# A graph network on one core: chunk bases of the next stage set earlier, node groups half a turn nearer to their edges

## The reference

```python
h = jnp.maximum(_layernorm(x), 0.0); x = x + L0(h, edges, edge_attr_64)      # edge MLP, summed by node
h = jnp.maximum(_layernorm(x), 0.0); x = x + L1(h, src, dst, edge_type_8)    # typed messages, GRU per node
h = jnp.maximum(_layernorm(x), 0.0); x = x + L2(h, src, dst, edge_attr_8)    # pair interaction, summed by node
h = jnp.maximum(_layernorm(x), 0.0); x = x + L3(h, edge_index)               # two mean-aggregation layers

# L2, per edge
p1    = tanh(p @ pp_W1 + pp_b1) @ pp_W2 + pp_b2
inter = ((concat([p1[i], p1[j]]) @ pi_W1 + pi_b1) @ pi_W2 + pi_b2) @ pi_W3   # 64 x 8 values per edge
i1    = einsum('ecb,eb->ec', inter, basis)
i1    = tanh(i1 @ ii_W1 + ii_b1) @ ii_W2 + ii_b2
out   = segment_sum(i1, j)
```

## Time and profile before

| | us |
|---|---|
| median of three executions | 10330.74 |
| profiled execution | 10343.41 |
| its span | 10341.8 |
| PE busy | 5765.4 (56%) |
| DVE busy | 4372.1 (42%) |
| ACT busy | 2424.1 (23%) |
| POOL busy | 6918.9 (67%) |
| chain that ended last: POOL, PE, issue, DVE | 46%, 26%, 18%, 5% |

### The profile page before, as it was taken

One profiled execution on the slowest core, in us unless ns is written; L12 is line 12 of the kernel. 1 busy time (PEld: TensorE's weight loads), 2 busy tenths in 40 slices (PEclk: granted clock), 3 DMA queues, 4 the chain that ended last, 5 costly groups with the idle time before them and its releaser, 6 DMA issues.

```text
span 10341.8 us, 144754 instructions
## 1 busy us (share of the span) xinstructions
PE 5765.4 (56%) x32026; PEld 3576.5 (35%) x32026; DVE 4372.1 (42%) x11981; ACT 2424.1 (23%) x4618; POOL 6918.9 (67%) x7939
## 2 busy tenths in 40 slices
PE   6999996244444447999999962333333322222222
PEld 4777773222222223444444432222222211111111
DVE  6888886132323225777777751111111111111111
ACT  5999993000000002333333320000000000000000
POOL 3333331777777776777777757777777677777777
PEclk9999998555555558999999985555555555555555
DMA  3333333111111112222222211111111111111111
GB/s 104 96 97 96 97 97 118 27 29 30 29 30 29 30 29 51 61 61 61 61 61 60 60 37 27 28 28 28 28 28 28 24 27 28 28 28 28 28 28 27
DMA packets 503888, 488.54 MB, mean 47 GB/s; under 512 B 245340, under 2 KB 299425, under 8 KB 503777
## 3 DMA queue, kind: packets, MB, share of 16 engines
q0 software_dynamic: 220480, 235.58, 11.9%
q1 hardware_dynamic: 283360, 252.43, 8.4%
HBM read 427.04 MB, written 61.15 MB: 47 GB/s over the span
## 4 chain that ended last, share of the span: by engine, by line
POOL 46%; PE 26%; issue 18%; DVE 5%; ACT 1%; POOLq 1%; DVEq 1%; DMA 0%; ACTq 0%; SPq 0%
POOL mov L671 44%; PE ps L1527 5%; PE ps L1416 3%; PE ps L1390 3%; PE ps L1423 3%; PE ps L1519 3%; POOL outs L671 2%; PE ps L1546 1%; DVE scr L940 1%; PE ps L1512 1%; PE ps L1508 1%; PE ps L1537 1%; PE ps L1414 1%; PE ps L1452 1%; PE ps L1430 1%
## 5 line engine op out<-in xcount | busy, mean ns | idle before, releaser
L1390 PE MATMUL ps<-outs,mov 128*64 128x64 f32 x9984 | 1370.5, 319 | 4220.3 <-DMA mov<-tab_q,idx 1616.3
L1390 PEld LDWEIGHTS ps<-outs,mov 128*64 128x64 f32 x9984 | 1158.2, 221 | 4548.1 <-issue 4548.1
L840 DVE TENSOR_TENSOR acc<-acc,ps 64x64 f32 (+1 forms) x1664 | 354.1, 213 | 4441.8 <-PE ps L1390 4439.5
L671 POOL DMA_INDIRECT mov<-tab_msg,idx x1664 | 1578.6, 949 | 665.7 <-issue 492.3
L671 POOL DMA_INDIRECT outs<-tab_u,idx x1664 | 1590.2, 956 | 582.1 <-issue 486.4
L671 POOL DMA_INDIRECT mov<-tab_h,idx x1664 | 1573.9, 946 | 574.8 <-issue 506.6
L671 POOL DMA_INDIRECT mov<-tab_q,idx x1664 | 1573.3, 945 | 543.1 <-issue 506.6
L940 DVE TENSOR_TENSOR scr<-ps,scr 128x512 f32<-128x512 f32 x1664 | 1063.1, 685 | 368.9 <-PE ps L1519 337.3
L1527 PE MATMUL ps<-scr,w_bas 128*64 128x512 f32 x3328 | 899.9, 619 | 0.0
L634 POOL TENSOR_TENSOR scr<-outs 128x128 f32<-128x128 f32 x416 | 191.8, 461 | 816.3 <-DVE outs L850 815.5
L850 DVE TENSOR_TENSOR outs<-rel,iota_w 128x256 f32<-128x256 f32 x1664 | 705.6, 424 | 43.1 <-issue 30.1
(11 more groups left out here) (217 smaller groups left out, 8426.4 us busy)
## 6 DMA issues: line engine op xcount, KB each, us to landing
mov<-in_dst_row SPq DMA_DIRECT2D x832, 128.0 KB, 2.7
mov<-in_ea_T SPq DMA_DIRECT2D x416, 128.0 KB, 2.5
tab_msg<-outs SPq DMA_DIRECT2D x104, 256.0 KB, 2.0
mov<-tab_msg,idx POOLq DMA_INDIRECT x1664
outs<-tab_u,idx POOLq DMA_INDIRECT x1664
mov<-tab_h,idx POOLq DMA_INDIRECT x1664
mov<-tab_q,idx POOLq DMA_INDIRECT x1664
win<-tab_g SPq DMA_DIRECT2D x416, 32.0 KB, 2.4
```

The lines of the kernel that those rows point to most:

```text
L671: nc.gpsimd.indirect_dma_start(out=gat(e, u)[:, k, :], out_offset=None, in_=table, in_offset=bass.IndirectOffsetOnAxis(ap=idx[:, u, k:k + ...
L840: nc.vector.tensor_tensor(into, into, bank(banks[u % len(banks)])[0:rows, 0:W], ALU.add) \
L1390: last = mm(bank(banks[u % len(banks)])[0:width, 0:W], values(u)[:, k, :], sel(e, u)[:, k, :], start=k == 0, stop=k == TL - 1)
```

## The change

The node groups are 4.5 turns behind their edges in place of 5. Group g is taken when chunk 8g + 36 has been added. Each engine's node turns begin a turn earlier and each piece stands 4 steps later in it (2 steps in stage 2), with a third member 1 where that reaches into the next turn. The first turn with pieces is written out ahead of the loop, since late pieces have no group yet in it.

`set_windows` for the next stage now runs at the end of each stage's steps, through `drained`, before the pieces that are left over; for stage 0 it runs before the wait for the stored table. Copies of LAST and KEEP are held for those pieces. It also runs at the end of stage 4. The clearing of `win` for stage 2 stands ahead of stage 1.

```diff
-        def chunk_loop(eng, stages, kind=None, base_lag=0, per=1, nodes=None):
+        def chunk_loop(eng, stages, kind=None, base_lag=0, per=1, nodes=None, drained=None):
...
             def pieces_at(it, u):
-                for at_step, piece in pieces:
-                    if at_step == u and (not isinstance(it, int) or it - from_turn < SG):
-                        piece(it - from_turn)
+                for at_step, piece, late in pieces:
+                    if at_step == u and (not isinstance(it, int) or 0 <= it - from_turn - late < SG):
+                        piece(it - (from_turn + late))
...
             if from_turn < ITERS:
-                with eng.Fori(from_turn, ITERS) as it:
+                turn(from_turn, True)
+                with eng.Fori(from_turn + 1, ITERS) as it:
                     turn(it, True)
...
+            if drained:
+                drained()
...
-            def set_windows(e, p):
-                w0 = dve.snap((P * e + p) * 8)
-                if e > 0:
+            def set_windows(w0, first=False, pairs=False):
+                if not first:
                     dve.wait_ge(window_order, w0)
+                    nc.vector.tensor_copy(flag[:, LAST_HELD], flag[:, LAST])
+                    nc.vector.tensor_copy(flag[:, KEEP_HELD], flag[:, KEEP])
...
                 dve.wait_ge(window_order, w0 + 8)
+                nc.vector.tensor_tensor(flag[:, AT], flag[:, AT], flag[:, KEEP], ALU.mult).then_inc(window_order, 1)
+                dve.wait_ge(window_order, w0 + 9)
                 dve.sem_inc(windowed, 1)
 
+            def next_windows(e, p):
+                set_windows(dve.snap((P * e + p) * 9 + 9), pairs=e in (1, 2))
+                held[0] = True
...
-                if e == 2:
+                if e == 1:
                     for s in range(2):
                         order(nc.vector.memset(win[s * D:(s + 1) * D, :, (1 - s) * D:(2 - s) * D], 0.0))
                 with dve.Fori(0, P) as p:
-                    set_windows(e, p)
-                    turns = WAIT_TURNS + (2 if e == 2 else 1)
+                    held[0] = False
+                    turns = WAIT_TURNS + (1 if e == 2 else 0)
                     chunk_loop(dve, make(p), mybir.EngineType.DVE, ADD_LAG[e], per=2 if e == 2 else 1,
-                               nodes=(turns, pieces(p)) if pieces else None)
+                               nodes=(turns, pieces(p)) if pieces else None, drained=lambda: next_windows(e, p))
...
-                return [(2, candidate), (3, update), (7, rows_uv)]
+                return [(6, candidate), (7, update), (3, rows_uv, 1)]
...
                     wait_flow(dve, f, "ordered", t0_, g, 0)
+                    dve.sem_inc(dve_turn, 1)
...
-                return [(2, result), (3, norm3)]
+                return [(4, result), (1, norm3, 1)]
...
-                return [(2, hidden), (6, rows_q)]
+                return [(6, hidden), (2, rows_q, 1)]
...
-                return [(1, result)]
+                return [(5, result)]
...
-                chunks = g * RING + WAIT_TURNS * RING if not isinstance(g, int) or (g + WAIT_TURNS) * RING < CH else CH
+                ahead = WAIT_TURNS * RING - RING // 2
+                chunks = g * RING + ahead if not isinstance(g, int) or g * RING + ahead < CH else CH
...
-                           nodes=(WAIT_TURNS + 2, [(1, result2)]))
+                           nodes=(WAIT_TURNS + 1, [(3, result2)]))
```

More of the change, by code:

```diff
@@ L89, in build_gnn @@
         cnt = sb("cnt", [P128, NB])
-        IS_BAD, IS_FIT, STEP, AT, TMP, LAST, KEEP = (slice(n, n + 1) for n in range(7))
+        IS_BAD, IS_FIT, STEP, AT, TMP, LAST, KEEP, LAST_HELD = (slice(n, n + 1) for n in range(8))
+        KEEP_HELD = TMP
         stat = sb("stat", [P128, 4, SB])
@@ L358, in chunk_loop @@
             from_turn, pieces = nodes or (ITERS, [])
+            pieces = [piece if len(piece) == 3 else (*piece, 0) for piece in pieces]
             def step(it, u, which, base):
@@ L399, in chunk_loop @@
                     pieces_at(ITERS + n // ring, ring)
+            if drained:
+                drained()
             if pieces:
-                for it in range(ITERS + last // ring, from_turn + SG):
+                for it in range(ITERS + last // ring, from_turn + SG + 1):
                     for u in range(last % ring if it == ITERS + last // ring else 0, ring + 1):
@@ L773, in norm, with last_flag, keep_flag @@
                                                op0=ALU.max, op1=ALU.mult).then_inc(normed, 1)
-            def set_windows(e, p):
-                w0 = dve.snap((P * e + p) * 8)
-                if e > 0:
+            held = [False]
+            def last_flag():
+                return LAST_HELD if held[0] else LAST
+            def keep_flag():
+                return KEEP_HELD if held[0] else KEEP
+            def set_windows(w0, first=False, pairs=False):
+                if not first:
                     dve.wait_ge(window_order, w0)
+                    nc.vector.tensor_copy(flag[:, LAST_HELD], flag[:, LAST])
+                    nc.vector.tensor_copy(flag[:, KEEP_HELD], flag[:, KEEP])
                 nc.vector.tensor_scalar(base_n[:, :], first_f[:, :], flag[:, IS_FIT], flag[:, AT], ALU.mult, ALU.add) \
@@ L982, in _ @@
             node_loop("T0", t0)
+            order(nc.vector.memset(flag[:, AT], 0.0))
+            set_windows(0, first=True)
             edge_phase(0, edge_mlp)
@@ L1073, in update @@
                     rows = x[:, bass.ds(g * SB, SB), :]
-                    nc.vector.scalar_tensor_tensor(out=rows, in0=delta, scalar=flag[:, LAST], in1=rows,
+                    nc.vector.scalar_tensor_tensor(out=rows, in0=delta, scalar=flag[:, last_flag()], in1=rows,
                                                    op0=ALU.mult, op1=ALU.add).then_inc(f.sems["ordered"], 1)
@@ L1122, in rows_q @@
                     rows = x[:, bass.ds(g * SB, SB), :]
-                    nc.vector.scalar_tensor_tensor(out=rows, in0=q[:, :, D:2 * D], scalar=flag[:, LAST], in1=rows,
+                    nc.vector.scalar_tensor_tensor(out=rows, in0=q[:, :, D:2 * D], scalar=flag[:, last_flag()], in1=rows,
                                                    op0=ALU.mult, op1=ALU.add).then_inc(f.sems["settled"], 1)
-                return [(2, hidden), (6, rows_q)]
+                return [(6, hidden), (2, rows_q, 1)]
             def out_pieces(p):
@@ L1445, in plain @@
                     chunk_loop(pe, [(0, sum_stage(e, p, D, lambda u: gat(e, u), gathered_here(e, p), range(4, 8)))],
-                               nodes=(WAIT_TURNS, pieces(pe.snap(p * SG))))
+                               nodes=(WAIT_TURNS - 1, pieces(pe.snap(p * SG))))
             def rows_msg(j, s):
```

19 lines of the change are left out of this document (9 added, 10 removed).

## The result

| | before | after |
|---|---|---|
| median of four executions, us | 10331.08 (10329.4 to 10331.79) | 10393.95 (10392.98 to 10394.91) |
| profiled execution | 10343.41 | 10394.91 |
| PE, DVE, POOL busy | 5765.4, 4372.1, 6918.9 | 5782.8, 4374.2, 6928.9 |
| share of the last chain: POOL, PE, issue, DVE | 46, 26, 18, 5% | 46, 24, 19, 6% |

The ratio is 1.0061 (95% interval 1.0048 to 1.0074): 63 us slower. Between the two profiled executions it is 51.5 us. Busy times say nothing of it; the stages do.

The account below looks back on a forecast made before the run. POOL's gathers were taken to bound stages 1, 3 and 4, PE and DVE stage 2's turns, with stage ends exposed. Ends -24.6 and turns +74 gave +49 us: 10393 profiled, 10380 median, range 10325 to 10402.

Parts of the forecast that it names:

- ahead of stage 1's first gather: Stage 0: `set_windows` runs while DVE waits for the store, gain 3 us.
- stage 1 to 2: Group 47's update starts 2.3 us earlier and clearing and `set_windows` behind the store go; gain 9 us, bounds 7 and 15.
- stage 2: 46 turns each 1.6 us longer, +74 us, bounds 23 and 87; the stage would take about 2240 us.
- stage 2 to 3: DVE's chain after the last edge sum, with one norm moved ahead; -2 us, bounds -6 and +4.
- stage 3: Gathers were to keep 40.0 us per turn, other DVE or PE work being covered; no change.
- stage 3 to 4: Group 48 starts 7 us earlier on ACT and 4.9 us behind the store go; gain 12 us, bounds 5 and 13.
- end: End of stage 4: `set_windows` for a stage that does not exist delays group 48's result, 1.4 us later.
- The turn: Stage 2's turn end: the result delays the load of the bases, 1.6 us per turn, 46 turns, +74 us.
- z7, result, branch, load, z0: DVE's order at stage 2's turn end: z0 starts 3.6 us after z7 in place of 2.04, 1.6 us later.
- my lower bound: Stage 2's turn end: if the load could start earlier, only the result's 0.51 us shows, 23 us in all.
- The rival that the load stays covered: Stage 2's turn end costs 0 to 0.5 us, so mainly the ends count: 10306 to 10330, middle 10316; chance 0.17.
- The ends: Stage ends: -9, -12, -2, -3, 0 and +1.4 sum to -24.6 us, bounds about -37 and -8.

Follow-up runs that it names:

- before_again: The kernel before the change, with nothing changed, run and profiled again on one chip with after_again; 10331.08 us.
- after_again: The changed kernel, with nothing further changed, run again beside before on one chip; 10394.81 us, ratio 1.0061 to before.
- r_wait: The changed kernel with the wait for the result's operations moved from the turn's end to the norm, a step later; 10351.86 us, ratio 1.0005 to before.
- lag_only: The changed kernel with `set_windows` back behind the store, node groups still 4.5 turns behind; 10411.53 us, ratio 1.0064 to before.
- win_only: The changed kernel with node groups back to 5 turns behind, keeping the early `set_windows`; 10340.31 us, ratio 0.9992 to before.
- pad: The changed kernel plus one copy nobody reads in `hidden` of stage 3, to move `sel` later; 10400.73 us, ratio 1.0052 to before.
- clear_later: The changed kernel with result a turn later, norm in three parts, stage 3's clearing moved to `rows_q`, unneeded bases after stage 4's last result; 10295.28 us, ratio 0.9951.
- r_late: The changed kernel with stage 2's result moved to the next turn, right in front of the norm; 10431.01 us, ratio 1.0087 to before.

## Why the prediction was right, and what it missed

The sign and the place were right, and the median of 10394 lies within the range, 14 above the 10380 forecast. It is also inside the forecast's own range of 10366 to 10395, but by 1 us, and that is luck: 12 of the 14 us are those of stage 3, for which the sum had nothing. Step by step, with the two kernels on one chip (before_again, after_again) beside the first pair of profiles:

| term, us | predicted | first pair | one chip |
|---|---|---|---|
| ahead of stage 1's first gather | -3 | -4.3 | +1.7 |
| stage 1's gathers | 0 | -1.7 | +0.5 |
| stage 1 to 2 | -9 | -8.7 | -8.9 |
| stage 2 | +74 | +70.8 | +69.8 |
| stage 2 to 3 | -2 | -1.0 | -0.5 |
| stage 3 | 0 | +10.5 | +12.2 |
| stage 3 to 4 | -12 | -12.8 | -12.8 |
| stage 4's gathers | 0 | -2.5 | -0.3 |
| end | +1.4 | +1.1 | +1.5 |
| sum | +49 | +51.4 | +63.2 |

The table cuts stage 2 at its last gather. Cut at the last edge sum, as in the prediction, it took 2239.7 us in the first pair (forecast: about 2240), 73.1 more than before, and from there to stage 3 it is 3.2 less (forecast: 2 less).

1. *The turn.* The step "z7, result, branch, load, z0" held: 3.75 against 3.6 between z7 and z0, 1.58 against 1.6 per turn. r_wait shows that the wait is the cause of 1.29 of it, and not the operations. In r_wait at most 0.29 of the 0.51 of `result` shows, less than my lower bound. The rival that the load stays covered was wrong for this kernel for the reason given, the wait at the branch. Without that wait it holds: in r_wait the branch begins at 5067.5, before z7 (to 5068.09) and `result` (5068.01 to 5068.61), and the load at 5068.0. The rule of the Trainium skill ("Advanced Engine Details and Errata", Sequencer Loop) that engine instructions are read and queued while control code executes agrees with that.

2. *The ends.* 9 and 12 came as 8.9 and 12.8, by the two effects named: lag_only and win_only split the 12.8 into 7.7 and 5.2. The end of stage 4 cost 1.1 to 1.5 against 1.4. The 3 us ahead of stage 1 came at the start of stage 0 and did not last: on one chip POOL's first work of stage 0 is 2.9 us earlier (150.9 against 153.9), and the first gather of stage 1 is 1.7 later; the first pair gives -4.3 there. The bounds of the ends were added wrongly too: the lower ones make -41 with the 3 us of stage 0, not -37. The forecast does not hang on it.

3. *Stage 3: missed.* "Stages 3 and 4 must keep 40.0 us per turn" failed for stage 3, by 12 us. I had read "Whatever DVE or PE do beside that in those stages is covered" from the earlier trace rows, in which the maximum of 1218 ns already stood beside a median of 946, and did not ask which gathers were so long. What I took for cover is a phase: `sel` starts 0.32 us after a gather in before and 0.04 after it in many turns of after, and pad, which moves `sel` and takes nothing away, loses 10 us of the 12. Why the phase differs also in win_only, where the pieces of stage 3 stand at the same steps as before, stays open: what the changed kernels share is the turn written out ahead of the loop and the longer reach of `pieces_at`, and neither was undone alone.

4. *The reference point.* I took the difference for the same on profile and median. The profile of before was 12.7 us above its median, about 7.5 by the pace of POOL in that execution and 4 ahead of stage 1, and that of after was not. With the 51.5 between the first profiles, this is what makes the measured 63.

## What to carry to other kernels

Before a piece is moved to the end of a loop's turn, look for a wait in it: a wait there holds back the branch and the register load behind it, and costs their whole length (1.3 us a turn here), while the same operations without it cost at most 0.3. Long pieces beside a tight pair of engines are cheaper in parts that fit the slack of a step: that turned 41.3 us turns into 40.3, while putting two pieces into one step cost the clock. And where one engine sets the pace, the median of its operations says nothing of the few that stand: look at the maximum and at what starts beside it.

## What was not expected of the hardware

- A gather issued by POOL stands while `sel`, a comparison of DVE with two inputs in SBUF, is running 0.11 us after the gather's start: some 0.35 us at most, and as a rule 0 if `sel` starts later (the exceptions are named above). More work on DVE in the right place made stage 3 shorter by 10 us against stage 4.
- POOL's step is not the same in each execution of the same code: 1250.3 or 1248.7 ns on the mean in stage 4 of before, which over the 4989 steps of stages 1, 3 and 4 is 8 us. Whole executions differ by more: beside pad, on one chip, before took 10330.9 us once and 10342.1 to 10349.2 eight times, and clear_later 10278.9 once and 10294.4 to 10296.3 four times. A single profile can so lie 16 us off its kernel's median.
- The register load of eight bases takes 1.84 to 1.87 us in the turns of stage 2 in all kernels, with the engine idle beside it (after) or busy (before); a single one took 1.41 in each of the five kernels with the norm in parts.
- In r_late PE's clock halved in single turns first, and then in every turn, of 44.4 us each, to the end of the loop, without a change in the program. That a late turn and the lower clock keep each other going is how I read it, and was not tested. Its six executions lie between 10393 and 10480 us, wider than those of any other changed kernel.
